# Class values of the causal attention as bf16 parts, head stacks loaded by groups of four heads, and the loops of the token stages written out

## The chip, the cores and the metric

One core of one Trainium2 chip runs the whole program. The metric is the device time of one execution, in microseconds (us). The kernel before took 2279.78 us (median of 3 runs, 2278.9 to 2284.18).

## The reference, cut to what matters

Eight images of 512 tokens pass through a tower: token projection, a sparse layer, causal ReLU attention with 16 heads, an MLP, an fp4 feed-forward layer, a state-space layer, a mixture of experts, and a last attention. Every image also has one class row, which stands before its tokens. The part that the change is about is the first attention:

```python
x = x0 + (LN(x0) @ sf)                 # sparse layer
q = (x @ wq.T + bq); k = ...; v = ...  # 16 heads of 16
scores = einsum('bhqd,bhkd->bhqk', q, k) / 4
att = relu(scores) * tril(ones)
att = att / (sum(att) + 1e-9)
ctx = einsum('bhqk,bhkd->bhqd', att, v)
```

The sequence is the class row followed by 512 tokens, so every query also sees the class row's key and value. The class row's key and value are the same for all images.

## The kernel before, in words

Tokens lie in 33 tiles of 128 rows: tile 0 holds the eight class rows, tiles 1 to 32 the tokens, four tiles to an image. The stages follow each other as blocks, and between two blocks all engines meet at a barrier: `pass_tokens`, `pass_qkv`, `pass_causal`, `pass_mlp`, `pass_fp4`, `pass_ssm_in`, `pass_scan`, `pass_moe`, `pass_attend`. Five of them (tokens, qkv, mlp, fp4, moe) walk over the tiles with the generator `tiles` (L57), whose first few tiles are straight code and whose rest is a hardware loop of two tiles. Each engine has its own copy of the loop; the order of the work on each engine is written by hand, and semaphores tie the engines together.

`pass_qkv` (L429): for each tile, POOL finishes the norm's scale (L406, L408), DVE applies it (L421), TensorE (PE) turns the tile (L495), multiplies by wq, wk (L505) and wv (L512), and ACT adds the bias (L559). The fp32 result of q and k is split into three bf16 parts whose sum is the fp32 number: ACT writes the first (L566), DVE the rest and the second (L622, L624), POOL the third (L588). SP stores the parts (L463) and v (L466) to DRAM. The parts have two buffers: ACT writes part 0 of tile s only when the store of tile s-2 has landed. The class row's key gives one more score per head and token (PE L523); ACT takes its ReLU as fp32 (L572), SP stores it to `cls_w` (L459).

`pass_causal` (L680) works through 8 images (batches) of 4 groups of 4 heads, with 4 key tiles to a group. SP loads a half of the heads of an image at a time (`load_half`, L665): 6 copies for q and 6 for k (L671), each of 16 partitions with 8 heads of 1024 bytes, one copy of v (L672) and one of the class scores (L674). The parts lie so that one bf16 multiplication over 96 rows (6 products of parts for 16 dimensions) gives an fp32-like score.

```python
def class_value(b, g):                                   # L746
    past(pe, s_ctxs, NG * b + g - 1)
    nc.tensor.matmul(ps[:, 4 + g % 2, :], vbd[:, HG * g:HG * (g + 1), :]...,   # L748, fp32
                     cls_w[:, g // 2, :], start=True, stop=False, ...)
```

PE's order in each step is: four score multiplications (L743), the transposes of the last group (L769, at key tile 2), the four value multiplications of the step before (L757, fp32, 17 columns each), and at key tile 0 the class value of the group (L748), which starts the sum in the group's bank. ACT takes the ReLU of heads 0 and 2 (L802) and POOL masks them (L833); DVE does both for heads 1 and 3 (L863). The block diagonal matrix `vbd` of the class row's values is built at the start of the stage, from `v_all`, `own` and `pick` (PE L732, DVE L854). SP reloads a half as soon as its two groups are done (wait on `s_pv`).

Of the kernel before, what the change touches and what calls it, by code (L numbers as in the profile page):

```python
# [33 lines left out]
P = 128  # L34
# [178 lines left out]
def pass_tokens(nc, env, io):  # L213
# [4 lines left out]
    with a.ctx:  # L218
# [23 lines left out]
        def _(sp):  # L242
# [7 lines left out]
            for s, u, n in tiles(sp):  # L250
                if known(s) == 0:
                    continue
                for half, used in enumerate((s_tok0, s_tok)):
                    if known(s) >= 3:
                        sp.wait_ge(used, s - 2)
                    ks = slice(half * KT // 2, (half + 1) * KT // 2)
                    sp.dma_start(xin[:, u, ks, :], io["xk"][s - 1, :, ks, :]).then_inc(s_xin[2 * half + u], 16)

        @block.tensor
        def _(pe):  # L260
# [37 lines left out]
            for s, u, n in tiles(pe, 5):  # L298
# [11 lines left out]
        def _(act):  # L310
# [8 lines left out]
            for s, u, n in tiles(act):  # L319
# [7 lines left out]
        def _(pool):  # L327
            pool.wait_ge(s_bc, 1)
            for s, u, n in tiles(pool):
# [17 lines left out]
        def _(dve):  # L347
# [18 lines left out]
            for s, u, n in tiles(dve, 5):  # L366
# [62 lines left out]
def pass_qkv(nc, env, io):  # L429
# [4 lines left out]
    with a.ctx:  # L434
# [13 lines left out]
        s_out, s_vout, s_cout = a.sems("out", 2), a.sems("vout", 2), a.sems("cout", 2)  # L448
        s_took = a.sem("took")
        cls_s = a.sb("cls_s", [NH, 2, P])  # L450
# [4 lines left out]
        def _(sp):  # L455
            def class_out(s, u):
                sp.wait_ge(s_cls, s)
                sp.sem_inc(s_took, 1)
                sp.dma_start(io["cls_w"][:, s - 1, :], cls_s[:, u, :]).then_inc(s_cout[u], 16)  # L459

            for s, u, n in tiles(sp, 5):
# [5 lines left out]
                if known(s) >= 1:  # L467
                    class_out(s, u)
# [4 lines left out]
            sp.wait_ge(s_cout[0], 16 * (NT // 2))  # L473
            sp.wait_ge(s_cout[1], 16 * (NT // 2))

        @block.tensor
        def _(pe):
# [49 lines left out]
            for s, u, n in tiles(pe, 5):  # L527
# [10 lines left out]
        def _(act):  # L538
# [29 lines left out]
            def take_class(s, u, n):  # L568
                act.wait_ge(s_c, s)
                if known(s) >= 3:  # L570
                    act.wait_ge(s_cout[u], 16 * (n - 1 + u))
                nc.scalar.activation(cls_s[:, u, :], ps[0:NH, 6 + u, 0:P], ACT.Relu).then_inc(s_cls, 1)  # L572

            for s, u, n in tiles(act, 5):
# [10 lines left out]
        def _(pool):  # L585
# [5 lines left out]
            for s, u, n in tiles(pool, 5):  # L591
                ln.on_pool(pool, s, u)
                if known(s) >= 3:
                    third(s - 3, 1 - u)
            for s in range(NT - 3, NT):
                third(s, s % 2)

        @block.vector
        def _(dve):
# [26 lines left out]
            def value(s, u, n):  # L626
                dve.wait_ge(s_v, s + 1)
                if known(s) >= 2:
                    dve.wait_ge(s_vout[u], 16 * n)
                nc.vector.tensor_tensor(v[:, u, :, 0:HD], ps[:, 4 + u, 0:D].rearrange("p (h d) -> p h d", d=HD),  # L630
# [12 lines left out]
            for s, u, n in tiles(dve, 5, 2):  # L643
# [14 lines left out]
HG = 4  # L658
# [6 lines left out]
def load_half(sp, io, b, half, qs, ks, v, cls_w, sem):  # L665

    heads = slice(half * HALF, (half + 1) * HALF)
    for c in range(len(PQ)):
        for m, dst, part in ((half, qs, PQ[c]), (2 + half, ks, PK[c])):
            src = io["qk_parts"][part, m, :, bass.ds(1 + TB * b, TB), :].rearrange("(h d) n t -> d h (n t)", d=HD)  # L670
            sp.dma_start(dst[c:HD * len(PQ):len(PQ), :, :], src).then_inc(sem, 16)  # L671
    sp.dma_start(v, io["v_all"][bass.ds(1 + TB * b, TB), :, heads.start * (HD + 1):heads.stop * (HD + 1)]  # L672
                 .rearrange("n p f -> p n f")).then_inc(sem, 16)
    sp.dma_start(cls_w, io["cls_w"][:, bass.ds(TB * b, TB), :].rearrange("h n t -> h (n t)")).then_inc(sem, 16)  # L674


LOADS = 2 * len(PQ) + 2


def pass_causal(nc, env, io):  # L680
# [4 lines left out]
    with a.ctx:  # L685
        qs = a.sb("qs", [R, 2, HALF, S], BF16)
        ks = a.sb("ks", [R, 2, HALF, S], BF16)
        v = a.sb("v", [P, 2, TB, HALF * (HD + 1)])
        cls_w = a.sb("cls_w", [NH, 2, S])
        v0 = a.sb("v0", [P, NH * (HD + 1)])  # L690
        vbd = a.sb("vbd", [NH, NH, 2 * HD])
        own = a.sb("own", [NH, NH, HD + 1])
        pick = a.sb("pick", [P, NH])
        causal = a.sb("causal", [P, S])
# [6 lines left out]
        s_w, s_z0, s_prod, s_c8, s_vps, s_vbd = (a.sem(n) for n in ("w", "z0", "prod", "c8", "vps", "vbd"))  # L701
        s_load = a.sems("load", 2)
# [6 lines left out]
        def _(sp):  # L709
            sp.dma_start(v0[:, :], io["v_all"][0]).then_inc(s_w, 16)  # L710
            sp.dma_start(own[:, :, :], io["own"].rearrange("h (g d) -> h g d", d=HD + 1)).then_inc(s_w, 16)
            sp.dma_start(pick[:, :], io["row_pick"][:, 0:NH]).then_inc(s_w, 16)
            sp.dma_start(causal[:, :], io["causal"]).then_inc(s_w, 16)
            for half in range(2):
                load_half(sp, io, 0, half, qs[:, half], ks[:, half], v[:, half], cls_w[:, half, :], s_load[half])
            env.ahead["mlp"].start(sp)
            with sp.Fori(1, B) as b:
                for half in range(2):

                    sp.wait_ge(s_pv, STEPS * (b - 1) + STEPS // 2 * (half + 1))  # L720
                    load_half(sp, io, b, half, qs[:, half], ks[:, half], v[:, half], cls_w[:, half, :], s_load[half])

        @block.tensor
        def _(pe):
# [6 lines left out]
            pe.wait_ge(s_w, 64)  # L731
# [1972 lines left out]
```

## Time and profile before

| | us |
|---|---|
| median of 3 runs | 2279.78 |
| the profiled execution, its time | 2278.18 |
| its span, first to last instruction | 2276.4 |
| PE busy | 2098.8 (92%) |
| DVE busy | 1594.1 (70%) |
| ACT busy | 907.1 (40%) |
| POOL busy | 737.6 (32%) |

The stages on the trace: tokens to 170 us, qkv from 180 to 314, causal attention from 314 to 553, mlp to 866, fp4 to 1190, state space and scan to 1380, mixture of experts to 1798, last attention to the end. The span and the time differ by 1.8 us, and the profiled execution is 1.6 us below the median.

### The profile page before, as it was taken

The page shows a single profiled execution, that of the slowest core. Times are in us where ns is not written, and L with a number is a line of the kernel's source. Part 1 is how long each engine was busy: PE and PEld are TensorE (multiplying, and loading weights), DVE is VectorE, ACT ScalarE, POOL GpSimd, SP SyncE. Part 2 cuts the span into 40 slices and gives each one's busy share as a digit, 9 for nine tenths or more (in the row PEclk, how much of TensorE's full clock was granted, in tenths as well). Part 3 has the DMA queues.
Part 4 walks back from the last instruction along what each step waited for, and adds up shares of the span by engine and source line. Part 5 has one row for each costly group of instructions (what it writes and reads, how often), then busy time and mean ns, then how long its engine had stood idle before and what let it go on. Part 6 is the DMA issues. An engine that isn't in the chain of part 4 may idle for free. (4 is left out here: it accounts for less than half of the span.)

```text
span 2276.4 us, 41030 instructions
## 1 busy us (share of the span) xinstructions
PE 2098.8 (92%) x11587; PEld 1337.9 (59%) x11587; DVE 1594.1 (70%) x4366; ACT 907.1 (40%) x2124; POOL 737.6 (32%) x1350
## 2 busy tenths in 40 slices
PE   7998969998999997999988958999999999999998
PEld 6886833333888885666663316888888523333332
DVE  3336846665677776888866856776777788888882
ACT  1114635553221223444433431222222157777777
POOL 3554525554333332333422101111111423333222
PEclk9998979998999999999998968999999779999999
DMA  4323665443000000000001010212214302232210
GB/s 135 114 90 86 152 181 144 138 133 108 1 0 0 0 0 14 1 0 0 0 24 37 9 31 20 48 37 47 46 38 125 89 10 76 81 95 78 76 44 20
DMA packets 215394, 132.43 MB, mean 58 GB/s; under 512 B 116675, under 2 KB 204309, under 8 KB 215317
## 3 DMA queue, kind: packets, MB, share of 16 engines
q1 hardware_dynamic: 215316, 131.50, 21.4%
q8 instruction: 36, 0.59, 0.1%
q14 instruction: 42, 0.34, 0.0%
HBM read 89.81 MB, written 41.25 MB: 58 GB/s over the span
## 5 line engine op out<-in xcount | busy, mean ns | idle before, releaser
L2547 DVE TENSOR_REDUCE attend_mx<-ps 128x1 f32<-128x512 f32 x512 | 320.9, 682 | 40.5 <-PE ps L2241 39.4
L2384 ACT ACTIVATE attend_w<-ps 128x512 f32<-128x512 f32 x512 | 280.6, 596 | 92.5 <-PE ps L2255 90.7
L1854 PE MATMUL ps<-keep_early,moe_zT 128*128 128x256 f32 x1056 | 243.4, 384 | 6.4 <-DVE keep_h L2009 4.4
L1854 PEld LDWEIGHTS ps<-keep_early,moe_zT 128*128 128x128 f32 x1056 | 196.5, 191 | 43.1 <-DVE keep_h L2009 18.6
L2241 PE MATMUL ps<-keep_x,keep_o 96*128 96x512 bf16 x512 | 209.8, 416 | 5.7 <-DVE attend_mx L2547 4.0
L2255 PE MATMUL ps<-keep_o,keep_x 99*128 99x512 bf16 x512 | 191.6, 384 | 2.7 <-ACT attend_w L2384 2.7
L2009 DVE SCALAR_TENSOR_TENSOR keep_h<-ps,moe_g,keep_h 128x256 f32 (+1 forms) x264 | 127.6, 483 | 61.5 <-PE ps L1854 53.2
L863 DVE SCALAR_TENSOR_TENSOR keep_early<-ps,causal_causal 128x512 f32<-128x512 f32 (+3 forms) x256 | 114.0, 486 | 80.2 <-PE ps L743 80.1
L2241 PEld LDWEIGHTS ps<-keep_x,keep_o 96*128 96x128 bf16 x512 | 50.3, 99 | 183.8 <-DVE attend_mx L2547 136.0
L833 POOL TENSOR_TENSOR keep_early<-keep_early,causal_causal 128x128 f32<-128x128 f32 x256 | 113.3, 458 | 128.7 <-ACT keep_early L802 127.7
L802 ACT ACTIVATE keep_early<-ps 128x512 f32<-128x512 f32 (+3 forms) x256 | 98.5, 435 | 126.3 <-PE ps L743 126.0
L2273 PE MATMUL ps<-attend_w,keep_early 128*17 128x512 f32 x1024 | 135.5, 598 | 0.0
L1072 PE MATMUL ps<-mlp_zT,keep_early 128*128 128x128 f32 x1056 | 127.7, 280 | 4.6 <-ACT mlp_zT L1114 4.6
L1072 PEld LDWEIGHTS ps<-mlp_zT,keep_early 128*128 128x128 f32 x1056 | 121.4, 193 | 12.3 <-ACT mlp_zT L1114 8.8
L276 PE MATMUL ps<-tok_W,tok_xin 128*128 128x256 f32 x512 | 122.5, 383 | 0.0
L1081 PE MATMUL ps<-keep_early,mlp_f 128*128 128x256 f32 x528 | 119.3, 379 | 0.0
L1081 PEld LDWEIGHTS ps<-keep_early,mlp_f 128*128 128x128 f32 x528 | 100.2, 190 | 13.6
L276 PEld LDWEIGHTS ps<-tok_W,tok_xin 128*128 128x128 f32 x512 | 96.0, 193 | 12.7 <-issue 0.7
L743 PE MATMUL ps<-causal_qs,causal_ks 96*128 96x256 bf16 (+3 forms) x512 | 93.8, 306 | 10.4 <-DMA causal_cls_w<-cls_w 9.9
L743 PEld LDWEIGHTS ps<-causal_qs,causal_ks 96*128 96x128 bf16 x512 | 37.5, 98 | 111.8 <-issue 57.8
L1274 PE MATMUL ps<-fp_wd,fp_hT 128*128 128x256 f32 x396 | 92.9, 385 | 2.8 <-ACT fp_hT L1306 2.8
L757 PE MATMUL ps<-keep_early,causal_v 128*17 128x512 f32 (+3 forms) x1024 | 95.2, 442 | 0.2 <-POOL keep_early L833 0.2
(332 smaller groups left out, 4064.2 us busy)
## 6 DMA issues: line engine op xcount, KB each, us to landing
tok_xin<-in_xk SPq DMA_DIRECT2D x64, 256.0 KB, 2.7
qk_parts<-qkv_parts SPq DMA_DIRECT2D x33, 384.0 KB, 3.2
qk_parts<-moe_parts SPq DMA_DIRECT2D x33, 384.0 KB, 3.2
causal_qs<-qk_parts SPq DMA_DIRECT2D x96, 128.0 KB, 2.7
causal_ks<-qk_parts SPq DMA_DIRECT2D x96, 128.0 KB, 2.7
keep_o<-qk_parts SPq DMA_DIRECT2D x96, 128.0 KB, 2.8
keep_x<-qk_parts SPq DMA_DIRECT2D x96, 128.0 KB, 2.8
v_all<-qkv_v SPq DMA_DIRECT2D x33, 136.0 KB, 3.1
```

The costliest lines, as they stand in the source:

```text
L276: last = nc.tensor.matmul(ps[:, u, 0:D], xin[:, u, k, :], W[:, k // KD, k % KD, :], start=(k == 0), stop=(k == KT - 1))
L743: nc.tensor.matmul(ps[:, j, kt * P:S], ks[:, half, hh + j, kt * P:(kt + 1) * P], qs[:, half, hh + j, kt * P:S], start=True, stop=True).the ...
L863: nc.vector.scalar_tensor_tensor(w[:, j, kt % 2, 0:S - kt * P], ps[:, j, kt * P:S], 0.0, causal[:, 0:S - kt * P], ALU.max, ALU.mult).then_ ...
L1072: last = nc.tensor.matmul(ps[:, bank, m * P:(m + 1) * P], f1[:, k, f0:f0 + P], zT[:, k * P:(k + 1) * P], start=(k == 0), stop=(k == KD - 1))
L1081: last = nc.tensor.matmul(ps[:, F2, 0:D], f[:, m, :], f2[:, m, :], start=(m == 0), stop=(m == KF - 1))
L1854: last = nc.tensor.matmul(ps[:, E0 + pair % 2, e % 2 * D:(e % 2 + 1) * D], zT[:, u, k * P:(k + 1) * P], we[e][:, k, :], start=(k == 0), st ...
L2009: ins = nc.vector.scalar_tensor_tensor(env.h[:, s, :], ps[:, E0 + pair % 2, e % 2 * D:(e % 2 + 1) * D], g[:, u, 3, e:e + 1], env.h[:, s, : ...
L2241: nc.tensor.matmul(ps[:, MX + i % RING, :], qs[0:R, x.buf(0), h, t * P:(t + 1) * P], ks[0:R, x.buf(0), h, :], start=True, stop=True).then_ ...
L2255: nc.tensor.matmul(ps[:, SC + i % RING, :], ks[:, x.buf(2), HG * g + j, kt * P:(kt + 1) * P], qs[:, x.buf(2), HG * g + j, :], start=True, ...
L2273: last = nc.tensor.matmul(ps[2 * HD * j:2 * HD * j + HD + 1, CTX, :], v[:, buf, kt, (HG * g + j) * (HD + 1):(HG * g + j + 1) * (HD + 1)], ...
L2384: nc.scalar.activation(w[:, j, kt % 2, :], ps[:, SC + (HG * k + j) % RING, :], ACT.Exp)\
L2547: nc.vector.tensor_reduce(mx[:, t, k:k + 1], ps[:, MX + (TB * k + t) % RING, :], AX, ALU.max)\
```

## The change

Three things are changed together.

Loops: `tiles` has no hardware loop any more; all 33 tiles are straight code on each engine in the tokens, qkv, mlp, fp4 and moe stages (and for the POOL norm of the state-space stage), and the 8 batches of the causal attention are written out as well.

Class scores and values: the class scores are split into three bf16 parts in `pass_qkv`. ACT writes the fp32 ReLU and part 0, POOL the rest, part 1 and part 2 (three operations on 16 partitions by 128 columns, four tiles late), and SP stores them as six rows per head with three copies. The value of the class row is split once, on POOL, and stored into a zeroed block diagonal area in DRAM. The class value becomes a bf16 multiplication over 48 rows.

Loads: a half of q and k stacks is loaded as two quarters of four heads, 12 copies to a quarter, each quarter as soon as its group's last scores are done; v and the class scores come in two copies once the half's values are done. The first half of image 0, the causal mask and the block diagonal values are loaded during `pass_qkv`, from tile 27 on; SP's instructions for that stand between the stores of tiles 27, 28 and 29.

```diff
-def tiles(eng, peeled=3, tail=0):
-    for s in range(peeled):
-        yield s, s % 2, s // 2
-    with eng.Fori(0, (NT - peeled - tail) // 2) as i:
-        yield 2 * i + peeled, 1, i + peeled // 2
-        yield 2 * i + peeled + 1, 0, i + peeled // 2 + 1
-    for s in range(NT - tail, NT):
+def tiles():
+    for s in range(NT):
         yield s, s % 2, s // 2
 # pass_qkv, SP
             def class_out(s, u):
-                sp.wait_ge(s_cls, s)
-                sp.dma_start(io["cls_w"][:, s - 1, :], cls_s[:, u, :]).then_inc(s_cout[u], 16)
+                sp.wait_ge(s_clsp, s)
+                for part in range(3):
+                    at, n = PQ.index(part), PQ.count(part)
+                    sp.dma_start(io["cls_parts"][:, at:at + n, s - 1, :],
+                                 cls_p[:, s % 4, part:part + 1, :].to_broadcast([NH, n, P])).then_inc(s_cout[s % 4], 16)
...
-                if known(s) >= 1:
-                    class_out(s, u)
+                if known(s) >= 2:
+                    class_out(s - 1, 1 - u)
+                if isinstance(s, int) and s == 4:
+                    class_value_rows()
+                if isinstance(s, int) and s == NT - LATE:
+                    for w in range(2):
+                        sp.wait_ge(s_out[w], 16 * 3)
+                        sp.wait_ge(s_vout[w], 16 * 3)
+                    for w in range(4):
+                        sp.wait_ge(s_cout[w], 48)
+                    ahead.first.load_stacks(sp, io, 0, 0)
+                    ahead.first.load_stacks(sp, io, 0, 1)
+                if isinstance(s, int) and s == NT - LATE + 1:
+                    sp.wait_ge(s_diag, 16 * 6)
+                    ahead.first.load_values(sp, io, 0)
+                    ahead.load_constants(sp, io)
 # pass_qkv, ACT
-                nc.scalar.activation(cls_s[:, u, :], ps[0:NH, 6 + u, 0:P], ACT.Relu).then_inc(s_cls, 1)
+                nc.scalar.activation(cls_s[:, s % 4, :], ps[0:NH, 6 + u, 0:P], ACT.Relu)
+                nc.scalar.activation(cls_p[:, s % 4, 0, :], ps[0:NH, 6 + u, 0:P], ACT.Relu).then_inc(s_cls, 1)
 # pass_qkv, POOL
+            def class_parts(s):
+                u = s % 4
+                ch = Chain(pool, c_cls, 2 * (s - 1))
+                pool.wait_ge(s_cls, s)
+                pool.sem_inc(s_took, 1)
+                ch.link(nc.gpsimd.tensor_tensor(cls_r[:, :], cls_s[:, u, :], cls_p[:, u, 0, :], ALU.subtract))
+                pool.sem_inc(s_took, 1)
+                ch.link(nc.gpsimd.tensor_copy(cls_p[:, u, 1, :], cls_r[:, :]))
+                pool.sem_inc(s_took, 1)
+                nc.gpsimd.tensor_tensor(cls_p[:, u, 2, :], cls_r[:, :], cls_p[:, u, 1, :], ALU.subtract).then_inc(s_clsp, 1)
+                pool.wait_ge(s_clsp, s)
...
                 ln.on_pool(pool, s, u)
                 if known(s) >= 3:
                     third(s - 3, 1 - u)
+                if known(s) == 3:
+                    class_value()
+                if known(s) >= 5:
+                    class_parts(s - 4)
 # pass_causal
+    def load_stacks(self, sp, io, b, quarter):
+        at = quarter * HG
+        for c in range(len(PQ)):
+            for m, dst, part in ((self.n, self.qs, PQ[c]), (2 + self.n, self.ks, PK[c])):
+                src = io["qk_parts"][part, m, at * HD:(at + HG) * HD, bass.ds(1 + TB * b, TB), :]...
+                sp.dma_start(dst[c:HD * len(PQ):len(PQ), at:at + HG, :], src).then_inc(self.s_stacks[quarter], 16)
...
-            with sp.Fori(1, B) as b:
+            for b in range(1, B):
                 for half in range(2):
+                    for quarter in range(2):
+                        g = 2 * half + quarter
+                        sp.wait_ge(s_sc[HG - 1], STEPS * (b - 1) + TB * (g + 1))
+                        halves[half].load_stacks(sp, io, b, quarter)
                     sp.wait_ge(s_pv, STEPS * (b - 1) + STEPS // 2 * (half + 1))
-                    load_half(sp, io, b, half, ...)
+                    halves[half].load_values(sp, io, b)
...
             def class_value(b, g):
+                if g % 2 == 0:
+                    pe.wait_ge(s_values[g // 2], VALUES * (b + 1))
                 past(pe, s_ctxs, NG * b + g - 1)
-                nc.tensor.matmul(ps[:, 4 + g % 2, :], vbd[...], cls_w[:, g // 2, :], ...)
+                at = 2 * HD * HG * (g % 2)
+                nc.tensor.matmul(ps[:, 4 + g % 2, :], vb[:, g // 2, at:at + 2 * HD * HG], halves[g // 2].cls[:, :], ...)
```

The build of `vbd` (PE L732, DVE L839 and L854, the loads L710 to L713) falls away, and PE, POOL and DVE wait once for the mask and the block diagonal values. The class rows' own output (DVE L850) moves to the end of the stage.

## Rows read from the trace of the kernel before

**Rows 1.** Busy time by stretch: qkv, then causal (us, then engine busy, PEclk, DMA)

```profile
200.00:290.00 90.00, 90.00 (x660) 74.50 (x660) 76.26 (x178) 56.15 (x175) 53.92 (x77) 1.00 0.68 152
...
350.00:540.00 190.00, 187.98 (x1504) 67.78 (x1496) 125.13 (x389) 100.26 (x250) 98.19 (x223) 1.00 0.49 137
```

**Rows 2.** Groups of the causal stretch: the class value (count, then busy and mean ns)

```profile
L748 PE MATMUL ps<-causal_cls_w,causal_vbd 16*128 16x512 f32 x64 | 36.8, 655 | 0.0
```

**Rows 3.** Timeline of PE in the causal stretch: one group (start, us, operation)

```profile
442.44 1.12 PE L748 MATMUL ps<-causal_cls_w,causal_vbd 16*128 16x512 f32 x2
...
447.87 1.04 PE L743 MATMUL ps<-causal_qs,causal_ks 96*128 96x512 bf16 x4
448.84 0.41 PE L757 MATMUL ps<-keep_early,causal_v 128*17 128x128 f32 x8
449.18 1.12 PE L748 MATMUL ps<-causal_cls_w,causal_vbd 16*128 16x512 f32 x2
450.23 0.50 PE L743 MATMUL ps<-causal_qs,causal_ks 96*128 96x384 bf16 x2
```

**Rows 4.** Timeline between qkv and causal, PE and SP

```profile
306.12 0.60 PE L523 MATMUL ps<-qkv_qkf,keep_kbd 128*16 128x128 f32 x4 [0.73 <-ACT qkv_cls_s L572]
...
314.57 0.36 SPq L710 DMA_DIRECT2D causal_v<-v_all  x1
...
315.63 0.28 PE L728 MATMUL ps<-keep_head_mask,causal_prod 128*8 128x16 f32 x4 [8.91 <-DVEq L842]
...
324.89 0.50 SPq L674 DMA_DIRECT2D causal_cls_w<-cls_w  x1
...
328.00 1.86 PE L743 MATMUL ps<-causal_qs,causal_ks 96*128 96x512 bf16 x4 [8.36 <-DMA causal_cls_w<-cls_w]
```

**Rows 5.** Groups of POOL in the qkv stretch (200 to 290 us)

```profile
L408 POOL TENSOR_TENSOR qkv_rs<-qkv_ve,keep_mhalf 128x1 f32<-128x1 f32 x26 | 20.4, 786 | 2.0
```

**Rows 6.** Timeline of POOL and DVE in one qkv tile

```profile
259.98 1.01 POOL L408 TENSOR_TENSOR qkv_rs<-qkv_ve,keep_mhalf 128x1 f32<-128x1 f32 x1
...
260.53 0.43 DVE L624 CAST qkv_parts<-qkv_rest 128x512 bf16<-128x512 f32 x1
...
261.04 1.16 POOL L588 TENSOR_TENSOR qkv_parts<-qkv_rest,qkv_parts 128x512 bf16<-128x512 f32 x1
...
261.21 1.13 DVE L421 TENSOR_SCALAR qkv_z<-keep_x,qkv_mv,qkv_rs 128x256 f32 x1
```

**Rows 7.** Groups of POOL in the whole span (busy, mean ns, then idle before)

```profile
L833 POOL TENSOR_TENSOR keep_early<-keep_early,causal_causal 128x128 f32<-128x128 f32 x256 | 113.3, 458 | 128.7 <-ACT keep_early L802 127.7
...
L2415 POOL TENSOR_TENSOR attend_nrest<-keep_early,attend_nparts 16x512 f32<-16x512 f32 x16 | 18.5, 1156 | 1.3
...
L2417 POOL CAST attend_nparts<-attend_nrest 16x512 bf16<-16x512 f32 x16 | 9.7, 608 | 2.7 <-POOL attend_nrest L2415 2.7
```

**Rows 8.** SP's DMA issues, three kinds (start, us of the issues together, count)

```profile
323.61 0.60 SPq L671 DMA_DIRECT2D causal_ks<-qk_parts  x1
...
1198.06 1.38 SPq L1485 DMA_DIRECT2D ssm<-ssm_pr  x3
...
1806.02 2.10 SPq L2191 DMA_DIRECT2D attend_vb<-diag_parts  x6
```

**Rows 9.** Timeline of PE: the turn that opens each mlp tile

```profile
578.60 0.41 PE L1061 MATMUL ps<-keep_ident,mlp_z 128*128 128x128 f32 x2
587.46 0.40 PE L1061 MATMUL ps<-keep_ident,mlp_z 128*128 128x128 f32 x2
...
605.44 0.40 PE L1061 MATMUL ps<-keep_ident,mlp_z 128*128 128x128 f32 x2
```

**Rows 10.** Timeline of PE: the turn that opens each moe tile

```profile
1442.00 0.44 PE L1829 MATMUL ps<-keep_ident,moe_z 128*128 128x128 f32 x2
1454.13 0.44 PE L1829 MATMUL ps<-keep_ident,moe_z 128*128 128x128 f32 x2
...
1478.67 0.44 PE L1829 MATMUL ps<-keep_ident,moe_z 128*128 128x128 f32 x2
```

More of the change, by code:

```diff
@@ L662 @@
 PK = (0, 1, 2, 0, 1, 0)
[L665 to L674, printed above, removed]
@@ new lines, with __init__, reserve, load_constants @@
+STACKS, VALUES = 16 * 2 * len(PQ), 16 * 2
+class Causal:
+    def __init__(self, nc):
+        self.area = Area(nc, "first")
+        self.s_stacks, self.s_values = self.area.sems("stacks", NG), self.area.sems("values", 2)
+        self.s_const = self.area.sem("const")
+    def reserve(self):
+        self.first = Half(self.area, 0, self.s_stacks[0:2], self.s_values[0])
+        self.causal = self.area.sb("causal", [P, S])
+        self.vb = self.area.sb("vb", [HALF * len(PQ), 2, HALF * 2 * HD], BF16)
+    def load_constants(self, sp, io):
+        sp.dma_start(self.causal[:, :], io["causal"]).then_inc(self.s_const, 16)
+        for c, part in enumerate(PK):
+            sp.dma_start(self.vb[c:HALF * len(PK):len(PK), :, :],
+                         io["diag_parts"][part, 0, :, 0:HALF * HALF * 2 * HD].rearrange("a (h x) -> h a x", h=HALF))\
+                .then_inc(self.s_const, 16)
@@ L685, in pass_causal @@
     with a.ctx:
[L686 to L694, printed above, removed]
+        ahead = env.causal
+        halves = [ahead.first, Half(a, 1, ahead.s_stacks[2:4], ahead.s_values[1])]
+        s_stacks, s_values, s_const, causal, vb = ahead.s_stacks, ahead.s_values, ahead.s_const, ahead.causal, ahead.vb
+        v0 = a.sb("v0", [B, NH * (HD + 1)])
         prod = a.sb("prod", [P, KD, B])
@@ L789, in _ @@
             batch(0, first=True)
-            with pe.Fori(1, B) as b:
+            for b in range(1, B):
                 batch(b)
@@ L820, in _ @@
             batch(0, first=True)
-            with act.Fori(1, B) as b:
+            for b in range(1, B):
                 batch(b)
@@ L1275, in down @@
                 last.then_inc(s_dn, 1)
[L1277 removed]
+            for s, u, n in tiles():
                 turn_z(s)
@@ L1323, in _ @@
             apply(0, 0)
-            for s, u, n in tiles(act, 5, 2):
+            for s, u, n in tiles():
                 if known(s) >= 3:
@@ L1621, in _ @@
         def _(pool):
-            for s, u, n in tiles(pool):
+            for s, u, n in tiles():
                 ln.on_pool(pool, s, u)
@@ L1801, in _ @@
         def _(sp):
-            for s, u, n in tiles(sp, 5, LATE):
+            for s, u, n in tiles():
                 sp.wait_ge(s_p2, s + 1)
@@ L2613, in build @@
         for step in PASSES:
-            step(nc, env, io)
+            if step is pass_qkv:
+                env.causal = Causal(nc)
+                with env.causal.area.ctx:
+                    env.causal.reserve()
+                    pass_qkv(nc, env, io)
+                    pass_causal(nc, env, io)
+            elif step is not pass_causal:
+                step(nc, env, io)
 PASSES = [pass_constants, pass_tokens, pass_qkv, pass_causal, pass_mlp, pass_fp4, pass_ssm_in, pass_scan, pass_moe,
```

155 lines of the change are left out of this document (96 added, 59 removed).

## The prediction

> **What bounds the kernel now.** I read the page first (which engine is busy in which slice), then busy time by stretch, then the groups and one period of the stretches that the change touches, then the hand-over between them, and last SP's issues, since the change issues more of them. In the qkv stretch PE is busy for 90.0 of 90 us and POOL for 53.9; in the causal stretch PE is busy for 188.0 of 190 us, while DVE has 125, ACT 100 and POOL 98 [rows 1]. So both stages run at PE's pace at the full clock, and the others wait for it. Between the two stages PE stands: its last qkv work begins at 306.12, the causal stage's first issue is at 314.57, its first score at 328.00, and the wait that ends last there is for SP's 14th load of the first half, issued at 324.89 [rows 4]. These are the places where time can go, and they ask in turn: how much PE work goes away, how much of the hand-over goes away, and which of POOL and SP then takes PE's place.
>
> **The class value on PE, a gain.** It runs once per group of heads, 32 times, in two passes each [rows 2]. From its start to the next score it holds PE for 450.23 - 449.18 = 1.05 us [rows 3]. A bf16 multiplication with 512 columns costs (448.84 - 447.87) / 4 = 0.24 us [rows 3], and I take that; the fp32 price itself is the other bound. Saved: 32 x 0.81 = 25.9 us, if PE stays the bound. The group goes from 449.18 - 442.44 = 6.74 us [rows 3] to 5.93. DVE needs about 125 / 190 x 6.74 = 4.4 us of that, POOL 3.5, ACT 3.6 [rows 1]: all fit.
>
> **The start of causal, a gain.** The first load is at 314.57, the first score 13.4 us later [rows 4]. With the first half, the mask and the block diagonal values already there, what is left is the small class product, PE at 315.63 for 0.28 us [rows 4]: the first score can go some 1.3 us after the barrier. Saved: 12.1 us. Against it, the loads of image 1 now queue behind the mlp weights, 2.5 MB, sooner than they did: 1.5 us lost (0 to 5). The class rows' output at the end costs DVE one small operation, which I leave at 0 against the `vbd` build that falls away.
>
> **POOL in qkv, a loss.** A tile has 26 passes on PE (2 turns, 16, 4 and 4 for q and k, v, class scores), so the stretch holds 660 / 26 = 25.4 tiles of 3.55 us, and POOL is busy 53.9 / 25.4 = 2.12 us in each [rows 1]. The class parts add three operations per tile. A 16-row operation costs as much as a 128-row one (1156 ns against 1.16 us, both 512 columns) [rows 6, 7], so the two subtractions of 128 columns cost 0.458 each; the cast, 0.608 at 512 columns, costs about 0.24 by the same ratio [rows 7]. Each is chained with a wait and a counter between; that pattern leaves 2.7 / 16 = 0.17 us idle [rows 7], and there are four such places: 1.16 + 0.68 = 1.84, with the last wait nearer 1.8. So POOL needs 2.12 + 1.8 = 3.92 us and becomes the bound, 0.37 over PE. DVE adds to it: L408 takes 0.786 us in the mean [rows 5], and where it takes 1.01 it ends with DVE's cast, 260.53 + 0.43 [rows 6]; if it does so in every second tile, it takes 0.56 by itself. A POOL without gaps meets that cast (0.43) in nearly every tile and L421 too, so I take 4.3 us, +0.75 over the 26 tiles until the burst below = 19.5 us (bounds: 3.92, 10 us; 4.5, 24 us). The extra class ReLU on ACT and the four operations that split the class value (POOL, tile 3) add 2 us at the stage's beginning (0 to 4), the class parts of the last tiles, with their three copies behind the last wait, 2 us at its end (0 to 4).
>
> L421 tells the same from the other side: it takes 1.13 us, and ends 0.14 us after POOL's L588, started before it, has ended [rows 6]. The Trainium skill (SBUF — State Buffer, Who interferes with whom) has a rule for this: the two engines share a port pair under an exclusive lock, and the second to come waits the whole operation. The trace agrees for L421 and the cast.
>
> **SP in qkv, a loss.** At tile 27 SP issues 24 stack copies in a row, then six of other work and 9 more loads at tile 28. The store of tile 28 stands behind them; ACT needs it landed before it may write part 0 of tile 30, then DVE and POOL follow, and PE's end of stage with them. What one quarter copy costs in issue, the trace does not show. The present ones, 128 runs of 1024 bytes on 16 partitions, cost 0.64 us each (two issues from 323.61 to 324.89) [rows 4, 8]; small ones of other shapes cost 1.38 / 3 = 0.46 and 2.10 / 6 = 0.35 [rows 8]. A quarter copy has the partitions of the first and half its runs, so I take the middle of 0.35 and 0.64 less a little, 0.475. The burst then holds SP for 11.4 us, and little of it is covered, because the pair of buffers lets ACT run only two tiles ahead: 11.4 us (4, if most is covered at 0.35, to 15.4 at 0.64).
>
> **SP in causal, the doubtful cover.** SP issued 28 copies per image and will issue 52 (48 quarter copies, 4 others at 0.5). At 0.475 this is 24.8 us against PE's 4 x 5.93 = 23.7, nearly hidden: the first image's lead absorbs most of the 1.1 us per image, and I put it at 0. It is the one resource without slack.
>
> **The loops, a small gain.** A straight mlp tile takes 587.46 - 578.60 = 8.86 us, two in the loop 17.98 [rows 9]: 0.13 x 30 = 3.9 us. In moe a straight tile takes 12.13, two in the loop 24.54 [rows 10]: 0.14 x 28 = 3.9 us. Tokens and qkv show no such gap behind a busy PE; fp4 and the rest I leave at 0. Together 8 us (5 to 10). Straight code must also be fetched; the straight tiles already there are the faster ones, so I cost that at nothing.
>
> **The sum.** -25.9 - 12.1 + 1.5 + 19.5 + 2 + 2 + 11.4 - 8 = -9.6 us. From the profiled execution's 2278.2 that is 2268.6; it stands 1.6 below the median, so 2270.2, say 2270. With the favourable bounds of all terms, -25.9 - 12.1 + 10 + 4 - 10, about 2246; with the unfavourable ones, PE still the bound, about 2286.
>
> **Rivals.** First, and slower: **SP's issues bound the causal stage**. Place: the 12 copies of each group. At 0.64 each an image takes 48 x 0.64 + 2 = 32.7 us, 9.0 more than PE, and over seven images, less the lead, about 58 us more; with the longer burst the sum is -10 + 58 + 4 = +52, 2331. Each 0.01 us of issue costs 0.24 + 3.36 us, so from about 0.50 the change is no gain. For it: a quarter copy has the form of L671's, and of that form the trace shows this price alone. Against it: copies of small or few runs cost 0.35 to 0.46 [rows 8]. Chance 0.32.
>
> Second: **DVE and POOL lock each other for more of the tile**. If L622, DVE's subtraction with 512 columns (0.7 us, an estimate from the cast's 0.43 [rows 6] at a slower rate), blocked POOL as the cast does, a qkv tile would need 3.92 - 0.24 + 0.7 + 0.43 + 0.2 = 5.0 us, 1.45 over 3.55, 38 us instead of 19.5: 2289. The mean of L408 [rows 5], stretched by some 0.23 and not by 0.7, speaks against it. Chance 0.1. The skill's section above counts a DVE operation with two SBUF inputs among those that lock, which is this case.
>
> Third: **the causal group does not shrink by the whole 0.81**. The class value also gave DVE time to finish the 512 column step before the next scores; if half of it comes back as a wait, +13: 2283, no change. The other engines' shares [rows 1] speak against it. Chance 0.1.
>
> Fourth: **POOL and the burst are covered better** than I reckon, since PE is a tile ahead when POOL falls behind: about 2252. Chance 0.08.
>
> **How the numbers follow.** The forecast's own case has 0.40. About 0.3% (6.8 us) is what a measurement of this kernel can tell from no change. The forecast's case lies below that line in three cases of four (0.30), the fourth rival wholly (0.08), and the mild end of the first and third a little (0.07): faster 0.45. Same: 0.16, from the upper end of the forecast and the third rival. Slower: 0.39, from the first rival, the second, and my unfavourable bounds. Range: the forecast's own case is 2254 to 2284; up to 2322 it takes in two thirds of the first rival (issue up to about 0.61).
>
> **What would show it.** Right: L748's place takes 0.24 us, the causal group 5.9 to 6.0 us, first score about 1.3 us after the barrier; POOL busy over 90% of a qkv tile of 4.2 to 4.4 us with PE waiting for L421; a gap in SP's stores of 11 us after tile 27; mlp tiles at 8.86 us. Wrong: PE L743 waiting for DMA at the start of groups, with SP issuing without pause (first rival); a qkv tile that stays at 3.55 us; a quarter copy at 0.6 us or at 0.35 us.

## The result and the profile after

The changed kernel takes **2356.92 us** (median of 4 runs, 2356.62 to 2357.41) against 2280.76 us (median of 4 runs, 2278.9 to 2284.18): 1.0332 times the time of before, 95% interval 1.0314 to 1.035. It is 76 us slower. I had forecast 2270 with a range up to 2322, and given the mechanism that decided it, SP's issues as the bound of the causal stage, a chance of 0.32 and a price of 2331.

Where the time went, from the two traces. The columns are the start of PE's first and of its last operation in a stage, and the time between them, in us.

| stage | before | after | longer by |
|---|---|---|---|
| tokens | 15.7 to 170.9: 155.2 | 15.5 to 175.2: 159.7 | 4.5 |
| qkv | 173.3 to 306.4: 133.2 | 177.6 to 348.6: 170.9 | 37.7 |
| from qkv's last to causal's first | 9.2 | 13.3 | 4.1 |
| causal | 315.6 to 551.7: 236.1 | 361.9 to 639.9: 278.1 | 42.0 |
| mlp | 310.7 | 307.5 | -3.2 |
| fp4 | 321.4 | 320.6 | -0.8 |
| state space | 147.3 | 145.5 | -1.8 |
| moe | 412.0 | 408.9 | -3.1 |

The last attention begins 79.2 us later (1878.2 for 1799.0) and is itself unchanged. So the loss lies in two stages, and the written-out loops give a little back behind them.

First, busy time by stretch of the changed kernel, as in [rows 1] (PE, PE's weight loads, DVE, ACT, POOL, then the granted clock, DMA's share and GB/s):

```profile
200.00:290.00 90.00, 79.47 (x564) 65.17 (x563) 69.11 (x150) 51.33 (x170) 72.57 (x128) 0.98 0.52 134
...
400.00:620.00 220.00, 185.17 (x1378) 64.44 (x1378) 117.47 (x364) 94.32 (x233) 91.50 (x207) 0.84 0.44 113
```

PE had been full in both stages; now it is busy for 79.5 of 90 us in qkv and 185 of 220 in causal. In qkv POOL has gone from 54 to 73 us of 90. In causal no computing engine has taken PE's place: all are less busy, as shares of the stretch, than before. What bounds that stage must be outside this row, so I read next what PE waits for from 320 to 640 us, which takes in the end of qkv (us in total, times, longest):

```profile
PE ps L847 <- DMA causal_cls<-cls_parts: 26.9, 8, 5.3
PE ps L847 <- DMA first_cls<-cls_parts: 21.2, 7, 7.7
PE ps L826 <- DVEq L941: 12.9, 1, 12.9
PE ps L536 <- ACT qkv_zT L579: 12.3, 1, 12.3
PE ps L554 <- ACT qkv_cls_p L603: 6.5, 1, 6.5
```

The class value (L847) waits 15 times, 48.1 us in all, for the class scores. They come with the last of the 26 copies of a half (24 of q and k, one of v, one of the class scores), so this wait names the end of what SP has to issue. SP's own waits, from 380 to 600 us:

```profile
SPq L747 <- PE ps L839: 2.9, 7, 0.5
SPq L751 <- PE ps L856: 1.2, 2, 0.8
```

SP waits for 4.1 us in 220. It issues almost without pause, and PE follows it. Its issues in the causal stage and at the end of qkv (start, us of the issues together, count):

```profile
467.56 0.57 SPq L747 DMA_DIRECT2D causal_qs<-qk_parts  x1
468.18 0.60 SPq L747 DMA_DIRECT2D causal_ks<-qk_parts  x1
...
315.26 0.68 SPq L747 DMA_DIRECT2D first_qs<-qk_parts  x1
...
330.55 0.60 SPq L747 DMA_DIRECT2D first_ks<-qk_parts  x1
331.19 0.58 SPq L478 DMA_DIRECT2D qk_parts<-qkv_parts  x1
331.82 0.86 SPq L481 DMA_DIRECT2D v_all<-qkv_v  x1
332.81 1.77 SPq L463 DMA_DIRECT2D cls_parts<-qkv_cls_p  x3
...
336.11 4.18 SPq L775 DMA_DIRECT2D first_vb<-diag_parts  x6
340.33 0.44 SPq L478 DMA_DIRECT2D qk_parts<-qkv_parts  x1
```

A quarter copy costs 0.59 us and a gap of 0.05, as the half copy with twice the rows did [rows 4, 8]. The burst holds SP from 315.26 to 331.15, 15.9 us. The same lines show what I had not costed: the store of tile 28 goes out at 331.19, the store of tile 29 only at 340.33, since the nine copies of tile 28 (`first_v`, `first_cls`, the mask and six of `vb`) and the class stores lie between.

### The profile page after: what moved, and what is told of

The parts are those of the page before. It is cut to its first block and busy times, and to the rows that moved or that the text cites. A ratio compares the mean times of both kernels' runs of the same rounds, so it can differ in the third digit from the quotient of the medians.

```text
span 2355.2 us, 36516 instructions
## 1 busy us (share of the span) xinstructions
PE 2102.9 (89%) x11553; PEld 1340.5 (57%) x11553; DVE 1611.7 (68%) x4364; ACT 912.2 (39%) x2156; POOL 777.2 (33%) x1450
## 5 line engine op out<-in xcount | busy, mean ns | idle before, releaser
L1950 PEld LDWEIGHTS ps<-keep_early,moe_zT 128*128 128x128 f32 x1056 | 196.5, 191 | 40.0 <-DVE keep_h L2105 15.5
L955 DVE SCALAR_TENSOR_TENSOR keep_early<-ps,first_causal 128x512 f32<-128x512 f32 (+3 forms) x256 | 115.8, 486 | 124.5 <-PE ps L839 123.3
L2105 DVE SCALAR_TENSOR_TENSOR keep_h<-ps,moe_g,keep_h 128x256 f32<-128x256 f32 x264 | 127.5, 483 | 61.3 <-PE ps L1950 53.8
L933 POOL TENSOR_TENSOR keep_early<-keep_early,first_causal 128x128 f32<-128x128 f32 x256 | 113.4, 456 | 170.0 <-ACT keep_early L901 169.0
L271 PEld LDWEIGHTS ps<-tok_W,tok_xin 128*128 128x128 f32 x512 | 96.3, 193 | 12.8 <-issue 0.7
L401 POOL TENSOR_TENSOR moe_ve<-moe_mv,keep_eps 128x1 f32<-128x1 f32 x33 | 6.3, 190 | 266.5 <-DVE moe_mv L410 266.5
L1354 PE MATMUL ps<-fp_wg,fp_zT 128*128 128x352 f32 x264 | 86.1, 470 | 1.4 <-ACT fp_zT L1428 1.4
L1370 PEld LDWEIGHTS ps<-fp_wd,fp_hT 128*128 128x128 f32 x396 | 75.0, 190 | 18.4 <-ACT fp_hT L1402 3.6
```

The lines of the kernel that those rows point to most:

```text
L271: last = nc.tensor.matmul(ps[:, u, 0:D], xin[:, u, k, :], W[:, k // KD, k % KD, :], start=(k == 0), stop=(k == KT - 1))
L955: nc.vector.scalar_tensor_tensor(w[:, j, kt % 2, 0:S - kt * P], ps[:, j, kt * P:S], 0.0, causal[:, 0:S - kt * P], ALU.max, ALU.mult).then_ ...
L1370: last = nc.tensor.matmul(ps[:, DN, 0:D], hT[:, k, :], wd[:, k, :], start=(k == 0), stop=(k == KI - 1))
L1950: last = nc.tensor.matmul(ps[:, E0 + pair % 2, e % 2 * D:(e % 2 + 1) * D], zT[:, u, k * P:(k + 1) * P], we[e][:, k, :], start=(k == 0), st ...
L2105: ins = nc.vector.scalar_tensor_tensor(env.h[:, s, :], ps[:, E0 + pair % 2, e % 2 * D:(e % 2 + 1) * D], g[:, u, 3, e:e + 1], env.h[:, s, : ...
```

## The experiments

**Is it SP, and does a copy cost the same whatever it carries?** Two kernels ask this: one with half as many copies for the same bytes, one with the same number of copies for a quarter of the bytes.

```diff
 # e_halves: causal, SP, images 1 to 7
-                    for quarter in range(2):
-                        g = 2 * half + quarter
-                        sp.wait_ge(s_sc[HG - 1], STEPS * (b - 1) + TB * (g + 1))
-                        halves[half].load_stacks(sp, io, b, quarter)
+                    sp.wait_ge(s_sc[HG - 1], STEPS * (b - 1) + 2 * TB * (half + 1))
+                    halves[half].load_half_stacks(sp, io, b)   # 12 copies of 8 heads
...
 # e_onehead: load_stacks of images 1 to 7
-    src = io["qk_parts"][part, m, at * HD:(at + HG) * HD, ...]
-    sp.dma_start(dst[c:HD * len(PQ):len(PQ), at:at + HG, :], src)
+    src = io["qk_parts"][part, m, at * HD:(at + 1) * HD, ...]
+    sp.dma_start(dst[c:HD * len(PQ):len(PQ), at:at + 1, :], src)
```

> The changed kernel, but images 1 to 7 load their stacks by halves again: 24 copies of 8 heads to an image in place of 48 of 4 heads, each half after its last scores. Image 0 is loaded as in the changed kernel. Theory (SP's issues bound the causal stage, and a copy costs 0.64 us whatever it carries): SP needs 24 x 0.64 + 2.3 = 17.7 us per image, PE 4 x 5.93 = 23.7 becomes the bound again, seven images lose 33.5 - 23.7 = 9.8 us each, 69 us in all, about 2288 us (2282 to 2294); the start of the stage keeps its stalls. Rival (the transfers themselves bound the stage: the bytes are the same): about 2357, with each copy at 1.2 us. Second rival (PE's group does not shrink by the whole 0.81 us): a group of 6.3 us or more, 2300 or more.

> The changed kernel, but each quarter copy of images 1 to 7 carries one head in place of four, a quarter of the rows and bytes; the other three heads of images 1 to 7 keep what was loaded before, so that part of the attention is computed on old data. Theory (the issue price is one per copy): an issue stays at 0.59 us with a gap of 0.05, and the time stays within 5 us of 2357. Rival (the price goes by rows or bytes): issues fall to 0.4 us or less, the causal stage gets 40 us or more shorter, about 2310 or less.

Measured: e_halves 2291.51 us (1.0048 of the kernel before, 1.0032 to 1.0064), 65 us less than the changed kernel; e_onehead 2354.01 us in one run, 3 us less (it leaves three of four heads of images 1 to 7 on old data). Its issues, with one head to a copy:

```profile
434.11 0.59 SPq L755 DMA_DIRECT2D causal_ks<-qk_parts  x1
434.74 0.59 SPq L755 DMA_DIRECT2D causal_qs<-qk_parts  x1
```

And PE in e_halves, one group, followed by its busy time:

```profile
452.87 1.03 PE L843 MATMUL ps<-first_qs,first_ks 96*128 96x512 bf16 x4
453.83 0.41 PE L860 MATMUL ps<-keep_early,causal_v 128*17 128x128 f32 x8
454.17 0.39 PE L851 MATMUL ps<-first_cls,first_vb 48*128 48x512 bf16 x1
454.49 0.82 PE L843 MATMUL ps<-first_qs,first_ks 96*128 96x384 bf16 x4
...
458.87 1.04 PE L843 MATMUL ps<-first_qs,first_ks 96*128 96x512 bf16 x4
```

```profile
400.00:570.00 170.00, 169.35 (x1456) 62.41 (x1456) 122.00 (x382) 98.93 (x248) 96.45 (x220) 0.97 0.54 146
```

Three copy sizes, one price when issued in a row: 0.59 to 0.60 us with a gap of some 0.05 for one, four and eight heads. So it is the count of copies that bounds the changed kernel's causal stage; with 24 in place of 48 to an image PE is full again (169.35 of 170 us), and a group takes 458.87 - 452.87 = 6.00 us. In the changed kernel the causal stage took 278.1 us, here 211.3. The rival that the transfers bound the stage is out: a quarter of the bytes changed next to nothing, and half the copies with all the bytes gave 65 us.

**What is the class value worth?** e_halves again, with an fp32 multiplication of the same shape.

```diff
-    nc.tensor.matmul(ps[...], vb[:, g // 2, at:at + 2 * HD * HG], halves[g // 2].cls[:, :], ...)
+    nc.tensor.matmul(ps[...], vb32[:, :], cls32[:, :], ...)   # zeroed fp32 tiles
```

> The kernel of e_halves (2291.5 us) with the class value as an fp32 multiplication of the same size (48 rows, 512 columns) on operands that are set to zero, so the class row's value is left out. Theory (where SP is not the bound, the class value's price on PE counts in full): 32 x (1.05 - 0.32) = 23 us longer, 2315 us (2311 to 2319). Rival (half of it or more lies under waits for other engines): 2303 or less.

Measured: 2314.17 us, 22.7 more than e_halves. The two were measured at different times, and the kernel before took 2279.46 us beside e_halves and 2282.65 beside this one, so some 3 us of the 22.7 may not be the class value's. In the traces the causal stage is 230.2 us for 211.3, 18.9 longer. Its group on PE:

```profile
452.33 1.12 PE L853 MATMUL ps<-causal_cls,causal_vb 48*128 48x512 f32 x2
453.39 0.82 PE L845 MATMUL ps<-causal_qs,causal_ks 96*128 96x384 bf16 x4
```

It holds PE for 453.39 - 452.33 = 1.06 us against 454.49 - 454.17 = 0.32 in bf16, and from the third image on a group takes 6.74 us for 6.01. So where SP is not the bound the bf16 form is worth its full price, 0.73 us a group, and DVE and the others leave nothing of it as a wait. For all 32 groups that would be 23 us. The 18.9 are some 26 groups' worth: in both kernels the first groups still wait for SP, whose loads of image 0's second half and of image 1 begin only with the stage. That the times differ by 22.7, almost the 32 x 0.73, is a coincidence. In the changed kernel itself the saving should be worth nothing, since PE waits at this very place for SP; no run tests that alone.

**What stretches a qkv tile?** The changed kernel without POOL's three operations on the class scores.

```diff
 # qkv, POOL
-                if known(s) >= 5:
-                    class_parts(s - 4)
...
 # qkv, SP
-                sp.wait_ge(s_clsp, s)
+                sp.wait_ge(s_cls, s)
```

> The changed kernel without the three POOL operations per tile on the class scores: parts 1 and 2 are left out (set to zero once) and SP stores them as before. Theory (POOL is what bounds a qkv tile): the tile goes back from 4.06 to 3.56 us, 14 us over 28 tiles, and the tail loses another 2: about 2341 us (2336 to 2346). Rival (SP's four stores per tile, or ACT's two class operations, are what stretches the tile): the tile stays at 4.06 us and the time at 2357, or moves by less than 5 us.

Measured: 2341.92 us, 15.0 less. Its tiles are 3.56 us in the steady stretch; in the traces qkv is 10.8 us shorter and the step from qkv to causal 4.1, back to the 9.2 us of the kernel before. POOL's groups in the changed kernel from 240 to 310 us (busy, mean ns, then idle before and who ended it), and a busy row of e_nopool for the same 70 us:

```profile
L619 POOL TENSOR_TENSOR qkv_parts<-qkv_rest,qkv_parts 128x512 bf16<-128x512 f32 x17 | 19.6, 1153 | 0.0
L631 POOL TENSOR_TENSOR qkv_cls_p<-qkv_cls_r,qkv_cls_p 16x128 bf16<-16x128 f32 x18 | 10.3, 573 | 3.2 <-POOL qkv_cls_p L629 3.2
L403 POOL TENSOR_TENSOR qkv_rs<-qkv_ve,keep_mhalf 128x1 f32<-128x1 f32 x18 | 10.0, 558 | 1.4
L629 POOL CAST qkv_cls_p<-qkv_cls_r 16x128 bf16<-16x128 f32 x17 | 8.4, 493 | 3.1 <-POOL qkv_cls_r L627 3.1
L627 POOL TENSOR_TENSOR qkv_cls_r<-qkv_cls_s,qkv_cls_p 16x128 f32<-16x128 f32 x17 | 8.0, 468 | 0.0
L401 POOL TENSOR_TENSOR qkv_ve<-qkv_mv,keep_eps 128x1 f32<-128x1 f32 x18 | 3.6, 200 | 4.4 <-POOL qkv_cls_p L631 4.4
```

```profile
240.00:310.00 70.00, 69.33 (x507) 57.11 (x507) 57.61 (x134) 46.56 (x154) 38.32 (x57) 1.00 0.59 150
```

POOL's operations add up to 59.9 us, and 12.1 us of idle time stand before them, nearly all of it the steps from one class operation to the next. Together that is a little over the 70 us, since the ends of operations overlap the next starts (1.2 us) and the first and the last reach beyond the stretch; inside it POOL is busy for 58.0 us. There is no slack left. Read the last numbers of each row together with the first: a page that says "POOL 83% busy" hides an engine that is the bound, because an idle time released by POOL itself is part of its chain. The theory holds: without the three operations PE is busy for 69.33 of 70 us.

**The burst before the causal stage.** One kernel spreads the 24 copies of image 0 over 24 tiles, one moves them into the causal stage.

```diff
 # e_spread: qkv, SP
-                if isinstance(s, int) and s == NT - LATE:
+                if isinstance(s, int) and s == NT - 24:
...
-                    ahead.first.load_stacks(sp, io, 0, 0)
-                    ahead.first.load_stacks(sp, io, 0, 1)
+                if s >= NT - 24:
+                    ahead.first.load_one_copy(sp, io, 0, s - (NT - 24))
 # e_start: qkv, SP
-                    ahead.first.load_stacks(sp, io, 0, 0)
-                    ahead.first.load_stacks(sp, io, 0, 1)
 # e_start: causal, SP, ahead of its first copy
+            halves[0].load_stacks(sp, io, 0, 0)
+            halves[0].load_stacks(sp, io, 0, 1)
```

> The changed kernel, but the 24 quarter copies of image 0 are issued one behind the stores of each tile from 9 to 32, in place of 24 in a row at tile 27; the nine copies of tile 28 stay in a row. Theory (the copies in a row hold back the stores of tile 28, and ACT, POOL and PE with them): the 12.3 us in which PE waits go away, less a few that the nine copies cost, so 10 to 15 us are saved: about 2344 us (2341 to 2348). Rival (what is late at the end of qkv is the class parts' own stores and POOL): less than 5 us saved, 2352 or more.

> The changed kernel, but the 24 quarter copies of image 0 are issued as the first of the causal stage. Theory (SP is what bounds both places, so its 24 x 0.64 = 15.4 us are only moved): qkv's end loses 13 to 16 us, the causal stage gains 15, the time stays within 5 us of 2357. Rival (PE bounds the causal stage apart from its start): the first score waits for 12 copies, 7.7 + 2 us, and the rest is covered: about 2350 or less.

Measured: e_spread 2352.79 us (2345.65 to 2356.51), e_start 2359.85 us (2356.52 to 2361.54). e_start did what was expected: qkv is 16.2 us shorter (154.7 for 170.9), causal 16.3 us longer (294.4 for 278.1). SP's time is only moved, and no PE work hides it in either place.

e_spread missed. Its qkv stage is 160.3 us, 10.6 shorter and thus in the range expected, but the time is only 4 less, in runs that differ by 11 (6 less by the ratios to the kernel before, which took 2282.65 us beside it). What is left at the end of qkv is visible in PE's waits from 315 to 360 us:

```profile
PE ps L833 <- DVEq L948: 14.5, 1, 14.5
PE ps L553 <- ACT qkv_cls_p L602: 9.5, 1, 9.5
```

PE still waits 9.5 us in qkv and 14.5 us from its last multiplication to the next stage: the nine copies of tile 28 (4.20 us for the six of `vb` alone) and the class stores, 1.8 us a tile when issued in a row, still stand before the last tiles' stores, and four of the 24 copies go out there too, from 331.79 to 347.22. That is a reading of the order of SP's issues; no run takes the nine copies or the stores away alone. The burst was the larger part, not the whole, of that end. Of the 10.6 us the trace gives back 1.7 in the step to the causal stage and 2.5 in it; another 1.1 and 1.6 are in mlp and state space, which this edit leaves alone and which differ by as much from trace to trace. So what e_spread is worth is not settled beyond "some us".

**The loops alone.** The kernel before with all loops over tiles and the causal stage's images written out, and the same with the tokens stage left as it was.

```diff
-    for s in range(peeled):
-        yield s, s % 2, s // 2
-    with eng.Fori(0, (NT - peeled - tail) // 2) as i:
...
+    for s in range(NT):
+        yield s, s % 2, s // 2
...
-            with pe.Fori(1, B) as b:
+            for b in range(1, B):
```

> The kernel before with all loops over tiles and over the images of the causal stage written out, nothing else. Theory after the changed kernel's trace: tokens 2 to 4.5 us longer, mlp 3, fp4 1, state space 2 and moe 3 us shorter, causal and qkv within 2: about 2275 us (2272 to 2279). Rival (the prediction's term): tokens unchanged, 8 us shorter, 2272 or less. Second rival (straight code must be fetched, and the fetches hold PE): slower than before.

> The kernel of e_loops (2273.9 us), but the loop of the tokens stage is kept as before. Theory (written out, DVE and POOL meet in the tokens stage and DVE's second operation on the tile takes 0.93 us in place of 0.35): that stage goes back from 158.9 to 155.2 us, 3.7 us less, about 2270 us (2267 to 2272). Rival (the stage's length depends on where things lie in memory or on fetching, not on the loop): unchanged, 2274.

Measured: e_loops 2273.87 us (0.9973 of before, 0.9963 to 0.9984), 5.6 us faster than the 2279.46 us beside it; e_tokloop 2271.85 us (0.9953, 0.9939 to 0.9966), where the kernel before took 2282.28. By the ratios the tokens loop is worth 0.2%, with intervals that overlap; by the traces its stage takes 158.9 us written out and 155.7 in the loop. DVE's second operation in it, in e_loops and then in e_tokloop:

```profile
L372 DVE TENSOR_SCALAR tok_z<-tok_x,tok_rs 128x256 f32<-128x256 f32 x13 | 12.1, 929 | 0.5
```

```profile
L385 DVE TENSOR_SCALAR tok_z<-tok_x,tok_rs 128x256 f32<-128x256 f32 x14 | 4.9, 353 | 0.5
```

The same operation takes 929 ns or 353. The timelines of the kernel before and of the changed one show what differs; DVE and POOL both read the tile that DVE has just finished:

```profile
140.91 0.35 DVE L380 TENSOR_SCALAR tok_z<-tok_x,tok_rs 128x256 f32<-128x256 f32 x1
...
141.05 0.81 POOL L344 TENSOR_TENSOR keep_x<-tok_x,tok_bias 128x256 f32 x1 [0.63 <-DVE tok_x L377]
```

```profile
139.24 0.93 DVE L375 TENSOR_SCALAR tok_z<-tok_x,tok_rs 128x256 f32<-128x256 f32 x1
139.28 0.73 POOL L339 TENSOR_TENSOR keep_x<-tok_x,tok_bias 128x256 f32<-128x256 f32 x1 [0.53 <-DVE tok_x L372]
```

In the loop POOL starts 0.14 us after DVE and DVE runs at its own pace, POOL taking 0.81. Written out, POOL starts 0.04 us after it, and DVE ends 0.16 us after POOL's 0.73 are over. The two cases do not mix: each tile of the traces is one or the other, and which it is goes with POOL's start, a tenth of a microsecond. What moves that start was not tested, but it is not DVE's own loop: in the kernel before DVE's first five tiles are straight code, those of POOL, ACT and SP only the first three, and it is the first three that have the long form. The third and the fourth tile of the kernel before:

```profile
32.43 0.93 DVE L380 TENSOR_SCALAR tok_z<-tok_x,tok_rs 128x256 f32<-128x256 f32 x1
37.16 0.35 DVE L380 TENSOR_SCALAR tok_z<-tok_x,tok_rs 128x256 f32<-128x256 f32 x1
```

So the trace from before already held this loss. With the loop kept (e_tokloop) the short form is back and the stage is 3.2 us shorter. The Trainium skill (SBUF — State Buffer, Who interferes with whom) says that whoever issues first gets the shared ports for the whole operation; the trace agrees in the second case, in that DVE ends only after POOL has ended, though by the starts on the trace DVE came first there too. In the first case POOL, the later one, takes only 0.07 us more than in the second, while DVE still runs for 0.21 us beside it: a hold for the whole of that isn't seen.

**A version that keeps what pays.** It has the bf16 class value; stacks by halves throughout; image 0's copies one to a tile; the class scores split once per image, one POOL operation of 512 columns to a tile; the tokens loop kept, the others written out. In e_best2 the class stores also go ahead of the tile's own.

```diff
 # qkv, POOL
-                if known(s) >= 5:
-                    class_parts(s - 4)           # 3 operations of 128 columns a tile
+                if s >= 8 and s % 4 < 3:
+                    class_part(s // 4 - 2, s % 4)  # 1 of 512 columns in 3 tiles of 4
 # qkv, SP
+                if 9 <= s < 21:
+                    ahead.first.load_half_copy(sp, io, 0, s - 9)
+                if s == 21:
+                    sp.wait_ge(s_cout[0], 48)
+                    ahead.first.load_values(sp, io, 0)
...
+                if 22 <= s < 29:
+                    ahead.load_constant(sp, io, s - 22)
 # causal, SP
-            halves[1].load_stacks(sp, io, 0, 0)
-            halves[1].load_stacks(sp, io, 0, 1)
+            halves[1].load_half_stacks(sp, io, 0)
...
```

> The bf16 class value with what bounded the changed kernel taken away: stacks by halves for all images; image 0's twelve copies one to a tile from tile 9 on, its values, mask and block diagonal one to a tile from 21 on; the class value's rows two copies to a tile; the class scores split once per image on 512 columns, one POOL operation to a tile, and stored once per image; the loop of the tokens stage kept. Theory (PE is the bound again in both stages): qkv as before the change, the causal stage 32 x 6.0 + 2 = 194 us against 236, the loops 9 us: about 2232 us (2226 to 2242). Rival (POOL's tiles with a 1.16 us operation more still stretch, 24 of them by 0.3 us and more, and the half loads come late): 2243 to 2255.

> The kernel of e_best (2242.9 us), but SP stores an image's class parts ahead of the tile's own stores, not behind them. Theory (at the end of qkv POOL's cast for image 7 waits 3.54 us for the store of image 6, which stands behind the last tile's stores): the end of qkv gets 3 us shorter, about 2240 us (2237 to 2243). Rival (the three copies delay the tile's own store, and ACT waits for that): unchanged or up to 5 us longer.

Measured: e_best 2242.88 us (0.9835 of before, 0.9817 to 0.9853), e_best2 2240.88 us (0.9815, 0.9801 to 0.9828), so 1.9% faster than the kernel before and 5% faster than the changed one. Busy time by stretch in e_best2:

```profile
240.00:300.00 60.00, 59.93 (x438) 49.30 (x437) 51.30 (x119) 41.03 (x136) 48.42 (x63) 1.00 0.73 188
350.00:510.00 160.00, 160.00 (x1415) 59.85 (x1411) 117.27 (x376) 94.06 (x240) 93.54 (x213) 1.00 0.55 152
```

PE is full in both stages. The causal stage takes 198.0 us against 236.1. These two kernels change several things at once, so they show that the parts fit together, not what each is worth. e_best came out 0.9 us above the theory's range, at the rival's lower edge: its qkv stage and the step to the next cost 137.2 + 12.3 us against 133.2 + 9.2, and POOL's wait at the end of it is this one:

```profile
316.82 0.60 POOL L649 CAST qkv_cls_p<-qkv_cls_r 16x512 bf16<-16x512 f32 x1 [3.54 <-DMA cls_parts<-qkv_cls_p]
```

e_best2 takes it off: 135.6 + 9.0 us. By the times the step is 2 us, with overlapping runs, so only the traces show it, and e_best2's trace is of one of its two runs near 2236 us, while the other three took 2240.9 to 2242.2.

## Why the prediction was wrong, step by step

**The step that failed: "a quarter copy has the partitions of the first and half its runs, so I take ... 0.475".** It is 0.59 + 0.05 = 0.64 us. I had the row that said so, L671 at 0.64 [rows 4, 8], and interpolated between it and copies of other shapes, on the thought that half the rows cost less. e_onehead shows that in a row of copies of this shape they don't cost less at all. Why the other shapes do is not shown, and it is not their size alone: six copies of 64 KB take 2.10 us [rows 8], and six of 8 KB 4.18 in the changed kernel's `first_vb`. With 0.475 SP needed 24.8 us per image against PE's 23.7 and I put the cover at 0; with 0.64 it needs over 32. The term "SP in causal", 0 in the sum, thus fails with it: the stage is 42.0 us longer where the sum had it 36.5 shorter (-25.9 - 12.1 + 1.5), and with half the copies (e_halves) it is 66.8 us shorter again. The prediction named 0.50 as the point from which the change is no gain, so the whole sign hung on a price without a row of its own, and the nearest form should have been taken, not the middle.

**The first rival was right in mechanism and short in size**: 2331 for 2357. Of the 26 us, the causal stage has 20: I reckoned 32.7 us of SP per image, and it is 34.0 (from one issue of the first half's class scores, 399.56, to the same six images later, 603.50), about 9 us in seven images, and I credited a lead of PE that was not there, since image 0's second half was itself late. The qkv end and the loops, the tokens stage above all, hold the rest. Two sums of the prediction were also slightly off: its unfavourable bounds add up to 2289, not 2286, and this rival to 2332.

**The class value**: right in kind, 0.32 us for 0.24 as its place, and 6.00 us for 5.93 as the group. It is worth 0.73 us a group (e_value32) for 0.81, 23 us for 25.9, but only once SP is out of the way. The third rival, half of it coming back as a wait, is refuted.

**The start of causal**: SP's first copy there is at 361.31 and the first score at 362.06, 0.75 us, where I said 1.3. The 12 us are there. But the time from PE's last qkv operation to that copy grew from 314.57 - 306.44 = 8.1 to 361.31 - 348.55 = 12.8 us, through the class parts of the last tiles, for which I had put 2. e_nopool shows that it is POOL's part of them: without it, and with the same stores, the step to the next stage is 9.2 us again.

**POOL in qkv**: right. A tile takes (319.87 - 242.91) / 19 = 4.05 us between PE's turns, I said 4.3 and gave 3.92 as the bound. Taking POOL's work away gives 15.0 us, for 19.5 + part of the 4: 10.8 in the stage and 4.1 behind it. The second rival, 5.0 us a tile, did not come.

**A part that I did not cost**: the six copies of the class value's rows behind tile 4. SP issues them in 4.05 us, from 219.89 to 223.94, ACT waits 3.2 us for a store behind them, and two tiles take 5.6 and 5.2 us, 3.7 us over two of 3.56 and 2.7 over two of 4.05. It is the same error as the burst in small.

**SP in qkv**: 24 x 0.475 = 11.4 us forecast; from the last turn to PE's last start the stage takes 28.7 us for 8.1, 20.6 longer. Of this the burst is 15.9 by SP's issues (16.2 by e_start's stage), and the rest was read as the nine copies and stores behind it. A part of it I had not counted at all: PE stands for 12.3 us, the granted clock is 0.5 from 327 to 340 us, the lower of its two levels, and the 16 multiplications that follow the wait (L536, at 335.78) take 3.78 us for 1.95 in the tile before.

**The loops**: 5.6 us for 8. mlp and moe gave 2.6 and 3.0 in e_loops, fp4 and state space 2.0 together and causal 2.5, but the tokens stage lost 3.7. I had looked there for gaps on PE and found none, and so called it safe; what changed was not a gap. And "the straight tiles already there are the faster ones" holds for mlp and moe, but not for tokens, where the straight ones had the slow DVE operation.

## What to carry to other kernels

Count the copies that a queue must issue per unit of work and multiply by the dearest row of the same form before any gain on an engine is booked: splitting each load in two doubled the issues here, and with 0.64 us each the queue became the bound at once. When an engine takes over small work, add its waits between dependent operations (here 0.17 to 0.24 us each), batch it over tiles, and spread loads for a later stage one to a tile instead of in a row before stores that others wait for. Where two engines read the same tile at once, writing out a loop made one operation 2.6 times as long here, so a neutral rewrite is measured too.

## What was not expected of the hardware

- In a row of copies of one shape the price of an issue does not depend on what the copy carries: 0.59 to 0.60 us of SP with 0.05 between, for 16 partitions with one, four or eight runs of 1024 bytes. Issued one to a tile it is otherwise: the quarter copies of e_spread take 0.57 us, but ten of the twelve half copies of e_best2 take 0.83 to 0.98.
- Now and then one issue of such a row takes up to three times as long (417.20, 1.22 us; 321.71, 1.15 us): 11 of the 384 quarter copies of the changed kernel, 8 us together over the usual price. e_halves and e_onehead have such issues too. The cause was not looked into; it makes an image on SP longer than 48 x 0.64 + 2.3 says.
- The granted clock of the causal stage is 0.84 in the changed kernel, where PE keeps stopping for SP, and 1.00 before. It can cost little there while SP is the bound, since SP waits for PE for only 4.1 us in 220; no run shows the price.
- POOL's cast of 16 x 128 (L629) takes 0.28 us in ten of 17 tiles and 0.84 in six, 0.49 in the mean; L631 takes 0.42 or 0.65, 0.57 in the mean. The long ones lie beside DVE operations for their whole length, but the short ones overlap DVE too, so what holds the long ones is not shown.
